# Row and column sums of the residual image, taken by channel halves, the first half behind its own addition

## What is computed

```python
x = x + _L0_conv_ref(_gn(x), ...)   # attention: 4 heads in 2x2 windows, 4 heads over pooled keys
x = x + _L1_conv_ref(_gn(x), ...)   # masked image, relu, 3x3 convolution, bias
```

```python
sumX = jnp.maximum(x.sum((2, 3)), 1e-09)
mu_x = jnp.maximum(jnp.round((ix * x).sum((2, 3)) / sumX), 1.0)
mu_y = jnp.maximum(jnp.round((iy * x).sum((2, 3)) / sumX), 1.0)
...
m = jnp.abs(posX - mu_x[:, :, None, None]) + jnp.abs(posY - mu_y[:, :, None, None])
m = 1.0 - m * mask_weight.reshape(1, depth, 1, 1)
m = jnp.maximum(m, -1.0)
m = jnp.where(filt.reshape(1, depth, 1, 1) == 1.0, m, 1.0)
...
x_relu = jnp.maximum(x * mask, 0.0)
out = lax.conv_general_dilated(x_relu, weight, ...)   # 3x3, padding 1
```

## Time and profile before

| | |
|---|---|
| median of 3 runs | 371.55 us |
| lowest, highest | 371.24, 372.12 us |
| the profiled execution, its own time | 373.09 us |
| its span (first to last instruction) | 371.2 us |
| mean granted TensorE clock | 0.922 |
| TensorE (PE) busy | 327.7 us, 88% of the span |
| DVE busy | 274.9 us, 74% |
| ScalarE (ACT) busy | 143.5 us, 39% |
| GpSimd (POOL) busy | 101.9 us, 27% |
| DMA, mean | 55 GB/s |

### The profile page before, as it was taken

How to read it: one execution, slowest core, us unless ns; L and a number is a source line. 1 busy time by engine, 2 the same in 40 slices (tenths; PEclk the granted TensorE clock), 3 DMA queues, 4 the chain that set the end, 5 groups by cost and what they waited for, 6 DMA issues and landing times.

```text
span 371.2 us, 4118 instructions
## 1 busy us (share of the span) xinstructions
PE 327.7 (88%) x1546; PEld 232.1 (63%) x1546; DVE 274.9 (74%) x512; ACT 143.5 (39%) x180; POOL 101.9 (27%) x59
## 2 busy tenths in 40 slices
PE   1797486899979499999899999998999999989995
PEld 1475434336854387378677783686868746868884
DVE  4962725997895858698887986789779857997662
ACT  1422433453570664346304884454046342131300
POOL 0454999900067002000490020002910200202000
PEclk9999556699969689999899999998999999999999
DMA  7659700002940000009901110079000000101002
GB/s 262 254 72 128 239 6 0 0 2 36 128 51 2 2 0 3 0 2 155 114 2 60 57 59 0 2 139 128 2 6 38 21 0 0 58 0 57 2 0 114
DMA packets 10340, 20.39 MB, mean 55 GB/s; under 512 B 1872, under 2 KB 4816, under 8 KB 10064
## 3 DMA queue, kind: packets, MB, share of 16 engines
q1 hardware_dynamic: 10320, 20.13, 26.4%
HBM read 7.93 MB, written 4.19 MB: 33 GB/s over the span
## 4 chain that ended last, share of the span: by engine, by line
PE 57%; DVE 20%; DMA 9%; ACT 6%; issue 4%; SPq 3%; DVEq 0%
PE slot L962 25%; PE cps L994 16%; PE slot L1038 7%; DMA ks<-probs 4%; PE cps L962 4%; DMA qs<-probs 3%; ACT probs L504 3%; DVE l_max L745 2%; PE cps L1038 2%; SPq L257 1%; PE slot L1163 1%; DVE v_lo L727 1%; DMA xy<-x 1%; DVE xn L940 1%; SPq L261 1%
## 5 line engine op out<-in xcount | busy, mean ns | idle before, releaser
L333 POOL TENSOR_TENSOR probs<-q_w,k_w 128x1024 f32<-128x1024 f32 x16 | 37.5, 2375 | 111.4 <-DVE rw L690 106.1
L994 PE MATMUL cps<-v_hi,cw_hi 128*128 128x512 f32 (+1 forms) x144 | 58.6, 407 | 3.8 <-DVE v_lo L727 3.6
L994 PE MATMUL cps<-v_hi,cw_lo 128*128 128x512 f32 (+1 forms) x144 | 58.2, 404 | 0.0
L994 PE MATMUL cps<-v_lo,cw_hi 128*128 128x512 f32 (+1 forms) x144 | 57.3, 398 | 0.0
L745 DVE TENSOR_REDUCE l_max<-slot 128x4 f32<-128x1024 f32 x32 | 37.7, 1219 | 18.5 <-PE slot L962 18.5
L504 ACT ACTIVATE probs<-slot 128x1024 f32<-128x1024 f32 x32 | 31.6, 1024 | 20.2 <-PE slot L962 20.1
L994 PEld LDWEIGHTS cps<-v_hi,cw_hi 128*128 128x128 f32 x144 | 28.2, 196 | 14.2 <-ACT v_hi L498 4.3
L962 PE MATMUL slot<-ks,qs 96*128 96x256 f32 x128 | 25.0, 344 | 11.3 <-DMA ks<-probs 4.9
L994 PEld LDWEIGHTS cps<-v_hi,cw_lo 128*128 128x128 f32 x144 | 27.9, 194 | 6.3 <-issue 0.7
L962 PEld LDWEIGHTS slot<-ks,qs 96*128 96x128 f32 x128 | 21.9, 237 | 15.2 <-DVE l_max L745 6.7
L994 PEld LDWEIGHTS cps<-v_lo,cw_hi 128*128 128x128 f32 x144 | 28.0, 194 | 4.9
(11 more groups left out here) (173 smaller groups left out, 637.6 us busy)
## 6 DMA issues: line engine op xcount, KB each, us to landing
qs<-probs SPq DMA_DIRECT2D x24, 256.0 KB, 7.4
xy<-x SPq DMA_DIRECT2D x8, 512.0 KB, 8.0
out<-xy SPq DMA_DIRECT2D x8, 512.0 KB, 2.8
raw_cw<-conv_w SPq DMA_DIRECT2D x2, 1152.0 KB, 6.6
ks<-probs SPq DMA_DIRECT2D x12, 128.0 KB, 7.1
probs<-h_qkv SPq DMA_DIRECT2D x2, 192.0 KB, 4.6
probs<-l_kv SPq DMA_DIRECT2D x2, 128.0 KB, 4.1
probs<-selectors SPq DMA_DIRECT2D x1, 256.0 KB, 4.0
```

The source lines that it names most:

```text
L333: nc.gpsimd.tensor_tensor(qk[:, j].rearrange("p (n w) -> p n w", n=NW), q_w[:].rearrange("p (n w) -> p n w", n=NW), k_w[:, j * G:(j + 1) * ...
L994: ins = nc.tensor.matmul(cps[:, pos % 2, y0 * WT:y1 * WT], (cw_hi, cw_hi, cw_lo)[part][:, k, pos, dy + 1, o * P:(o + 1) * P], (v_hi, v_lo, ...
```

## The change

`line_sums` now does one channel half, k. The half 0 is summed in `step(b)` right behind `residual(b, 0, 1)`, ahead of L878 (`k_w`), with `mask[:, 0]` as temporary. The half 1 is summed where both were, in `masks`, with `mask[:, 1]` as temporary. The semaphore `fold_c` now also counts the last addition of half 0, and `mask_parts` waits for it. The last image's two calls keep their place and their temporary.

```diff
--- before.py
+++ after.py
@@ -633,27 +633,27 @@
                 link(nc.vector.tensor_copy(pool_hi[:], pool_s))
                 link(nc.vector.tensor_tensor(pool_lo[:], pool_s, pool_hi[:].bitcast(F32), ALU.subtract))
 
-            def line_sums(b, at=slice(0, KT), done=mask_c):
+            def line_sums(b, k, done):
 
                 carry()
-                n = at.stop - at.start
-                y = img(b, at.start, 0, n * HW).rearrange("p (k n) -> p k n", k=n)
-                link = Chain(dve, fold_c, N_FOLD, b + at.start)
-                if done is mask_c:
-                    dve.wait_ge(pool_c, min(b + 2, B) * N_POOL)
-                    t = xn[:, at]
+                at, last = slice(k, k + 1), b == B - 1
+                link = Chain(dve, fold_c, N_FOLD, 0)
+                link.base = b * (2 * N_FOLD + 1) + k * (N_FOLD if last else N_FOLD + 1)
+                if last:
+                    dve.wait_ge(lnorm, B)
+                    t = v_w[:]
                 else:
-                    dve.wait_ge(lnorm, B)
-                    wait_count(dve, fold_c, link.base)
-                    t = v_w[:].unsqueeze(1)
-                w = HW // 2
-                nc.vector.tensor_reduce(rc[:, at, 0], y.rearrange("p k (h w) -> p k h w", h=H), AX_X, ALU.add)
-                link(nc.vector.tensor_tensor(t[:, :, 0:w], y[:, :, 0:w], y[:, :, w:2 * w], ALU.add))
+                    dve.wait_ge(v_dve, b * POS)
+                    t = mask[:, k]
+                wait_count(dve, fold_c, link.base)
+                y, w = img(b, k), HW // 2
+                nc.vector.tensor_reduce(rc[:, k, 0], y.rearrange("p (h w) -> p h w", h=H), AX_X, ALU.add)
+                link(nc.vector.tensor_tensor(t[:, 0:w], y[:, 0:w], y[:, w:2 * w], ALU.add))
                 while w > 2 * W:
                     w //= 2
-                    link(nc.vector.tensor_tensor(t[:, :, 0:w], t[:, :, 0:w], t[:, :, w:2 * w], ALU.add))
+                    link(nc.vector.tensor_tensor(t[:, 0:w], t[:, 0:w], t[:, w:2 * w], ALU.add))
                 dve.wait_ge(fold_c, link.base + N_FOLD)
-                nc.vector.tensor_tensor(rc[:, at, 1], t[:, :, 0:W], t[:, :, W:2 * W], ALU.add).then_inc(done, 1)
+                nc.vector.tensor_tensor(rc[:, k, 1], t[:, 0:W], t[:, W:2 * W], ALU.add).then_inc(done, 1)
 
             def mask_parts(b, at=slice(0, KT), done=None):
 
@@ -661,6 +661,8 @@
                 link = Chain(dve, mask_c, N_MASK, b) if done is None else Chain(dve, done, N_MASK, 0)
                 link.n = 1
                 dve.wait_ge(link.sem, link.base + 1)
+                if done is None:
+                    dve.wait_ge(fold_c, (b + 1) * (2 * N_FOLD + 1))
                 g, sums, parts, m = gn[1][:, :, at], rc[:, at], rw[:, at], mu[:, at]
                 both = [t.rearrange("p k s n -> p (k s) n") for t in (sums, parts)]
                 sx = g[:, 2:4]
@@ -801,7 +803,8 @@
             def masks(b):
 
                 dve.wait_ge(y_ready, (b + 1) * KT)
-                line_sums(b)
+                dve.wait_ge(pool_c, (b + 2) * N_POOL)
+                line_sums(b, 1, mask_c)
                 normalisation(b, 1)
 
             def front(b, older=None, first=False):
@@ -873,6 +876,8 @@
                 link(nc.vector.transpose(blocks, inv.unsqueeze(2).to_broadcast([P, HW // HD, HD])))
                 if not last:
                     residual(b, 0, 1)
+                    dve.wait_ge(y_ready, b * KT + 1)
+                    line_sums(b, 0, fold_c)
                 dve.wait_ge(blocks_c, (b + 1) * N_BLOCKS)
                 dve.wait_ge(lpv_pe, b + 1)
                 nc.vector.tensor_tensor(k_w[:], flat[0], v_w[:], ALU.mult).then_inc(lnorm, 1)
@@ -893,14 +898,14 @@
                 b, older = B - 1, B - 2
                 dve.wait_ge(y_ready, B * KT)
                 conv_result(older, (V_LEFT, V_RIGHT))
-                line_sums(b, slice(0, 1), mask_last[0])
+                line_sums(b, 0, mask_last[0])
                 mask_parts(b, slice(0, 1), mask_last[0])
                 conv_result(older, (POS + V_SUM,))
                 last_normalisation(1)
                 masked_image(b, 0)
                 conv_result(older, (POS + V_DIFF,))
                 conv_tiles(b, 0, 0)
-                line_sums(b, slice(1, 2), mask_last[1])
+                line_sums(b, 1, mask_last[1])
                 conv_low(b, 0, 0)
                 conv_tiles(b, 0, 1)
                 conv_result(older, (POS + V_LEFT, POS + V_RIGHT))
```

## The result

The changed kernel takes 377.79 us, median of 6 runs (376.41 to 381.31), against 371.40 us for the kernel before (371.02 to 372.12, 6 runs): a ratio of 1.0174, 95% interval 1.0136 to 1.0212. That is 6.4 us slower. The forecast was 3.4 us slower, 375.0 us, with a range up to 376.6. The direction was right and the size was not; the median lies outside the range. The profiled execution is the shortest of the six: 376.41 us, with a span of 374.6. In the experiments the medians are over all executions, while the ratios leave out those in the slow state, single ones of 468.6, 531.8 and 715.2 us among them, so a median and a ratio need not match exactly.

What follows compares the result with a forecast made beforehand. The prediction took waits to bound the kernel: scores of steps 1 and 2 for the DMA, step 0's maxima on DVE. Its terms 1.4 + 1.0 + 1.0 = 3.4 us on 371.55 gave 375.0 us, range 372.8 to 376.6.

Steps and rivals of the forecast that it cites:

- What bounds each step: Steps 1 and 2: scores wait 1.83 us for the stacking transfers' DMA; step 0: DVE ends TensorE's wait for the maxima.
- One half costs 3.01 us: Sums of one half hold DVE 3.01 us, as in the last image; both halves together take 5.11 us.
- The lower bound: Least cost of a half, 2.56 us, for which the whole sum was put at some 1.9 us.
- Steps 1 and 2, 1.0 us each: Ahead of `k_w`: after DVE's idle 1.63 us and TensorE's 0.51 us cover, TensorE starts 0.96 us late; 2.0 us in all.
- the exposed weight load: Steps 1 and 2: the weight load running ahead of TensorE's wait for `k_w` may be exposed, between 0 and 0.2 us.
- The saving in `masks` that gives nothing: 2.10 us leave `masks`, but at most 0.42 us could be gained before the normalisation waits for TensorE's group means.
- Step 0, 1.4 us: Step 0: TensorE starts on `k_w` 1.59 us late, its delay grows to 1.78, and the normalisation starts 1.42 us later.
- TensorE reached it at 84.14, behind matmuls on constants: Step 0: TensorE reaches `k_w` at 84.14, so with `k_w` ending at 85.68 it starts only 1.59 us late.
- idle 0.24 us of DVE: Step 0: DVE idles 0.24 us ahead of `k_w`, so `k_w` starts 2.79 us later.
- Rival (c): Step 0: TensorE's 1.4 us idle time ahead of `k_w` lowers the clock, 1.7 us more, total 376.7 us; chance 12%.
- The adding-up to one trace: Whole kernel: 3.4 us read from the profiled execution (373.09 us, 376.5 expected) added to the median 371.55, giving 375.0 us.
- The pair 5.34 and 3.64 us for the same 32 matmuls: Sign that the clock may fall: 32 matmuls took 5.34 us behind a 1.59 us wait, 3.64 later; 1.7 us lost.

Runs made afterwards that it cites:

- experiment 4: The changed kernel with the move in step 0 alone, steps 1 and 2 summing both halves in `masks`: 375.92 us, ratio 1.0103 to the kernel before.
- experiment 7: The changed kernel with only the first half's reduction ahead of `k_w`, its five additions back in `masks`: 373.24 us, ratio 1.0011 to the kernel before.
- experiments 3 and 4: The changed kernel with the move in steps 1 and 2 alone (375.45 us, ratio 1.0104), and in step 0 alone (375.92 us, ratio 1.0103).

## Why the prediction was right and wrong

**What bounds each step: right.** The scores of steps 1 and 2 wait 1.89 and 1.97 us for the transfers in the changed kernel, and step 0's maxima are ended by DVE.

**One half costs 3.01 us: right.** `k_w` starts 3.00 us after the reduction in step 0 (80.87 to 83.87). The Trainium skill's table with 58 cycles, which the prediction quotes (VectorE: DVE Perf Modes, section "The TRN2 errata"), gave an estimated 2.46 us, and these traces do not agree with it. The lower bound was summed a little low: with 2.56 us for a half the three terms fall by 0.45 us each, to 2.05 us and not 1.9.

**Steps 1 and 2, 1.0 us each: right.** The later start of TensorE was forecast as 0.96 and is 1.02 us. Up to the scores it is 1.2 us; the 0.2 us may be the exposed weight load that was named as possible, which no run shows; over the whole period between the two `k_w` it is 0.95 and 1.3 us in the two traces. That is 2.0 to 2.4 us for the forecast 2.0.

**The saving in `masks` that gives nothing: right.** DVE waits 1.64 us for the group means in all three steps of the changed kernel.

**Step 0, 1.4 us: wrong.** The step that failed is "TensorE reached it at 84.14, behind matmuls on constants", together with the idle 0.24 us of DVE. Both are slack of one kind of execution. A longer stretch at 1.2 GHz, seen at 50 to 54 us, 30 us ahead, had made TensorE late, and what looked like 1.5 us of cover was its lateness, while DVE's residual came only 0.5 us later than in the second trace. In that second trace there is no cover, and the delay of the start is 3.1 us. In the four traced executions with all the sums of the half ahead of `k_w` in step 0, DVE starts `k_w` at 83.75 to 84.04. Of the eight with nothing there, four are early and DVE starts it at 80.59 to 80.80, the whole half earlier; the other four are late, and DVE waits 0.21 to 1.62 us for TensorE and starts it at 81.30 to 84.36. So the prediction read its trace rightly, and the cover is there in some executions and not in others. It was taken as belonging to the kernel.

**Rival (c), priced at 1.7 us and given 12%: its effect happened, not on its own premise.** It had the clock fall behind a wait of 1.4 us. Behind 1.47 us, in experiment 4, it did not. The waits of the changed kernel were 3.04 and 5.06 us, and the clock fell behind both, at 1.6 and 2.3 us on the way to the scores.

The terms can now be put together where DVE ends step 0, at the maxima. They begin at 107.48 and 108.36 us in the two traces of the changed kernel and at 103.14 in the second of before: 4.3 and 5.2 us later, made up of the 3.1 or 3.25 us of later start and the 1.6 or 2.3 us of clock, less 0.35 us of slack at the group means. Against the first trace of before, at 105.12, it is 2.4 and 3.2 us. With 2.0 to 2.4 for the other steps the sum is 6.3 to 7.6 us against the early execution. Measured were 6.4, with an interval from 5.1 to 7.9. That fits, but part of it is luck of the traces: between the scores of step 0 and the means of step 1 the changed kernel takes 149.66 - 104.62 = 45.0 and 152.80 - 105.50 = 47.3 us, and the kernel before 46.6 and 48.15, with the twelve matmuls on constants in it between 4.8 and 6.6 us. That this is the clock's doing fits, but no run isolates it, and experiment 7 shows that a delay of 2.8 us in step 0 of one trace can go with 0.4 us in the median. How much of the 6.4 us is step 0's on average stays open within the 2 us of experiments 3 and 4.

**The adding-up to one trace: wrong.** I noted that the profiled execution was 1.5 us above the median and treated this as an offset. The further traces show that its step 0 was of the late kind. The view that could have told was at hand in the pages: the slice at 46 to 56 us has 5 tenths of the clock in the earlier trace rows and 8 tenths in the changed kernel's page.

```profile
PEclk9999585898989989999999999999999999999999
```

The pair 5.34 and 3.64 us for the same 32 matmuls, quoted as a risk for the changed kernel, would not have told: it is 5.34 and 5.28 us in the two traces of before.

## What to carry to other kernels

Slack is only a cover if it is the engine's own and not lateness of the other side in that one execution: so read it in a second execution's trace, or look at whether the waiting engine ran at its full clock in the whole stretch ahead, here up to 30 us back; if it did not, take the cover as zero for the upper end of the sum. Work moved ahead of the instruction on which another engine waits is free up to the sum of both idle times (in steps 1 and 2 here, 1.14 us of 2.1), and beyond it costs one for one, and more where the clock falls behind the new wait; a piece that doesn't fit can be split or put behind the handover, where the consumer is a later stage. And before counting time saved, look for the next wait behind it: here 0.4 us stood ahead of a matmul that came no earlier.

## What had not been expected of the hardware

One kernel's executions differ by up to 5 us on one core (370.5 to 375.6 us for the kernel before in 22 of one set of 23, the last at 531.8), and the same 32 matmuls took 3.64 us, 5.28 to 5.34 us or, once, 6.38 us in the same place in different executions. A wait of 1.59 us stands ahead of 5.34 us in the first traces, and one of 1.56 or 1.57 us ahead of 3.64 in others. In the scores, behind 1.83 us of waiting, twelve matmuls took 2.38 us, and behind 1.89 us in the changed kernel 1.70. Ahead of `k_w` in step 0, waits of 3.04, 3.21 and 5.06 us were followed by a slow stretch and waits of 1.47 and 2.56 were not. So the length of the wait alone doesn't say whether the clock falls: 1.59 us was followed by a slow stretch, and 1.66 and 2.56 us were not. The Trainium skill, TensorE: Matmul & The Clock Gate, section "Part 1: The HAM clock gate", says that the number of slow matmuls at a kernel's start varies from run to run. This case's traces show the same in the middle of a kernel, with the pairs above.
